# A four-layer graph kernel: last two tiles of the attention layer taken block by block, one combined flag, and filler products in two pauses

## What is computed

```python
Wh = x @ W;  f1 = Wh @ a1;  f2 = Wh @ a2
e = leaky_relu(f1 + f2.T, 0.2)
att = softmax(where(adj > 0, e, -9e15), axis=-1)
x = layernorm(x + relu(att @ Wh))          # layer 2
# layer 3: products of (adj > 0), (adj < 0) and adj with x, then with weights
```

## Time and profile before

| | |
|---|---|
| median of 3 runs | 1427.51 us (1426.62 to 1429.61) |
| the profiled execution's own time | 1426.91 us |
| its span (first to last instruction) | 1425.2 us |
| mean granted clock of TensorE | 0.977 of 2.4 GHz |
| PE busy with products | 1332.1 us, 93% |
| PE idle between layer 2 and layer 3 | 6.08 us |
| PE idle before the turns of layer 2 | 6.29 us |
| PE idle before the first tile of layer 2 | 5.73 us |

### The profile page before, as it was taken

One profiled execution on the slowest core, in us unless ns is written; L12 is line 12 of the kernel. 1 busy time (PEld: TensorE's weight loads), 2 busy tenths in 40 slices (PEclk: granted clock), 3 DMA queues, 4 the chain that ended last, 5 costly groups with the idle time before them and its releaser, 6 DMA issues.

```text
span 1425.2 us, 11729 instructions
## 1 busy us (share of the span) xinstructions
PE 1332.1 (93%) x4294; PEld 677.7 (48%) x4294; DVE 922.3 (65%) x1277; ACT 554.7 (39%) x491; POOL 193.4 (14%) x211
## 2 busy tenths in 40 slices
PE   5889997899989999999999999999999999999993
PEld 4434444344444444455445455544445444544451
DVE  6978887888864000003225453799978987898576
ACT  7543324966730000000211111456565566455343
POOL 0000002000020000000000000225430233124211
PEclk8999997999999999999999999999999999999997
DMA  9899972000026667658667158698877987688301
GB/s 396 331 389 412 391 305 99 0 0 0 0 97 187 194 195 193 193 151 268 197 219 235 35 171 308 256 371 307 313 263 256 338 314 290 240 309 319 138 1 50
DMA packets 78150, 311.10 MB, mean 218 GB/s; under 512 B 8700, under 2 KB 20603, under 8 KB 61307
## 3 DMA queue, kind: packets, MB, share of 16 engines
q1 hardware_dynamic: 78075, 310.17, 61.2%
HBM read 306.71 MB, written 3.43 MB: 218 GB/s over the span
## 4 chain that ended last, share of the span: by engine, by line
PE 83%; DMA 7%; DVE 7%; ACT 2%; issue 1%; POOL 0%; ACTq 0%; DVEq 0%; POOLq 0%; SPq 0%
PE ps L1440 30%; PE ps L1241 10%; PE ps L1175 10%; PE ps L1278 10%; PE ps L1100 6%; DMA ring<-in_adjR 6%; PE ps L1235 5%; PE ps L1350 2%; PE ps L1461 1%; DVE arena L1560 1%; PE ps L1422 1%; PE ps L1259 1%; PE ps L1462 1%; DMA ring<-in_adjB 1%; PE ps L1215 1%; PE ps L1260 1%
## 5 line engine op out<-in xcount | busy, mean ns | idle before, releaser
L1440 PE MATMUL ps<-arena,x 128*128 128x512 f32 (+1 forms) x1092 | 438.9, 562 | 2.9 <-ACT shared L978 1.6
L1440 PEld LDWEIGHTS ps<-arena,x 128*128 128x128 f32 x1092 | 206.1, 190 | 231.4 <-issue 225.2
L971 ACT ACTIVATE arena<-arena,bench 128x3328 f32<-128x3328 bf16 x78 | 239.8, 3075 | 188.8 <-PE ps L1440 176.4
L2145 DVE TENSOR_TENSOR arena<-arena,ring 128x3328 f32<-128x3328 f32 x51 | 184.7, 3621 | 26.6 <-ACT arena L971 26.1
L1241 PE MATMUL ps<-ring,x 128*128 128x512 f32 (+1 forms) x364 | 176.1, 566 | 0.0
L1278 PE MATMUL ps<-ring,x 128*128 128x512 f32 (+1 forms) x364 | 149.5, 563 | 1.3 <-DMA ring<-in_adjB 1.3
L1100 PE MATMUL ps<-ring,bench 128*128 128x512 f32 x260 | 122.7, 607 | 15.0 <-DMA ring<-in_adjR 15.0
L1845 DVE SCALAR_TENSOR_TENSOR bench<-b,cols,ps 128x128 f32<-128x128 f32 x26 | 7.3, 344 | 182.1 <-PE ps L1215 182.1
L715 POOL TENSOR_TENSOR ring<-ring,nid 128x128 f32<-128x128 f32 x51 | 95.1, 1864 | 210.8 <-DMA ring<-in_adjR 210.8
L1235 PE MATMUL ps<-arena,shared 128*128 128x512 fp8e4 (+1 forms) x364 | 103.6, 366 | 6.1 <-DVE shared L1650 6.1
L2145 DVE TENSOR_TENSOR arena<-arena 128x3328 f32<-128x3328 f32 x27 | 98.0, 3631 | 13.5 <-ACT arena L971 13.1
(11 more groups left out here) (326 smaller groups left out, 1513.4 us busy)
## 6 DMA issues: line engine op xcount, KB each, us to landing
ring<-in_adjR SPq DMA_DIRECT2D x51, 1664.0 KB, 8.7
ring<-in_adjB SPq DMA_DIRECT2D x312, 256.0 KB, 3.0
arena<-in_adjR SPq DMA_DIRECT2D x27, 1664.0 KB, 8.8
ring<-in_adjR SPq DMA_DIRECT2D x25, 1280.0 KB, 8.5
shared<-in_adj SPq DMA_DIRECT2D x7, 1664.0 KB, 10.8
es<-in_adj SPq DMA_DIRECT2D x7, 1664.0 KB, 10.6
xT<-in_adj SPq DMA_DIRECT2D x6, 1664.0 KB, 13.3
y<-in_adj SPq DMA_DIRECT2D x6, 1664.0 KB, 13.1
```

Source lines behind the costliest of these rows:

```text
L971: A_(E[n % 3], below[n % 3], ACT.Exp, bias=tt_[:, t * HEADS + k:t * HEADS + k + 1], scale=-WIN).then_inc(e_exp, 1)
L1440: last = mm(ps[:, b, 0:w], lhsT=x[:, t], rhs=E[n % 3][:, o_:o_ + w], start=(t == 0), stop=(t == TILES - 1))
L2145: v.tensor_tensor(E[n % 3], E[n % 3], row_at(n), ALU.mult).then_inc(q_ready, 1)
```

## The change

It has four parts.

1. **Last two tiles.** Tiles 0 to 23 (`BY_TILE`) are taken as before. Tiles 24 and 25 are taken together, block by block, and behind each block from the second on stand two pairs of the W1 products. ACT makes all seven copies to `UT` and does its pairs in between (`RELU_BEHIND`). The buffers change place so that `shared` and the first half of the ring are free two and three tiles before the end. SP loads the first 6 chunks (`EARLY_CHUNKS`) after tile 22. POOL puts back the borrowed column of `x` in two pieces. `PART1` goes from 12 to 8 tiles, and only every other step of DVE's loop has a `norm_pair`.
2. **One flag.** DVE also computes the smaller of both flags (`BOTH`). PE asks that one before layer 2. If it is set, layer 2 and the start of layer 3 follow each other without another question and without a jump.
3. **Filler products before the turns:** 5 products of 512 columns into bank 3, whose results nobody reads, behind layer 1's last product.
4. **Filler products before layer 2:** 4 products into bank 7, behind the flag and POOL's `aside_done`.

```diff
-        EL = [piece(ring_flat, 0, NP), piece(ring_flat, NP, NP), es_flat, shared[:]]
+        turned_tile = [piece(ring_flat, 0, NP), piece(ring_flat, NP, NP)]
+        EL = [es_flat, turned_tile[1], turned_tile[0], shared[:]]
...
-        PART1, PART2 = 12, 24
+        PART1, PART2 = 8, 24
+        BY_TILE = TILES - 2
+        RELU_BEHIND = ((), (0, 1), (2, 3), (4, 5), (6, 7), (8,), (9, 10, 11, 12))
+        EARLY_CHUNKS = NP // CW
...
-        Z1_BANKS = (7, 0, 1, 2, 3, 4, 5, 7, 1, 3, 4, 5, 6)
+        Z1_BANKS = (7, 0, 1, 7, 2, 7, 3, 1, 4, 7, 5, 3, 6)
...
@@ SP, layer2 @@
+                    sp.wait_ge(used1, TILES - 3)
+                for t in range(EARLY_CHUNKS):
+                    ring_load(R2, t, 0, t, BLOCKS[0][1])
+                if not general:
                     sp.wait_ge(sums1, NB)
...
@@ ACT, layer2 @@
+                act.wait_ge(used1, BY_TILE)
                 for b, (o_, w) in enumerate(BLOCKS):
+                    act.wait_ge(sums1, b + 1)
+                    A_(UT[:, o_:o_ + w], ps[:, b, 0:w], ACT.Identity, bias=xsb).then_inc(ut1, 1)
+                    for k in RELU_BEHIND[b]:
+                        relu_pair(k)
+                        if k == PART1 // 2 + 1:
+                            roots(1, 0, PART1)
...
@@ PE, behind layer 1's products @@
+            def keep_busy(bank, rhs, times):
+                for _ in range(times):
+                    mm(ps[:, bank, :], lhsT=ident[:], rhs=rhs, start=True, stop=True)
+
+            keep_busy(3, xT[:, 0:MAX_WIDTH], 5)
...
@@ PE, layer2 @@
+                def products1(lo, hi):
+                    for k in range(lo, hi):
+                        pe.wait_ge(ut1, max(k // 2, Z1_BANKS[k] if Z1_BANKS[k] < NB else 0) + 1)
+                        if Z1_BEFORE[k] is not None:
+                            pe.wait_ge(z_out, 2 + GROUPS + Z1_BEFORE[k] + 1)
...
                     if t == 0:
                         pe.wait_ge(aside_done, 2)
+                        keep_busy(7, x[:, 0:BT].rearrange("p t f -> p (t f)"), 4)
...
+                for b, (o_, w) in enumerate(BLOCKS):
+                    for t in range(BY_TILE, TILES):
+                        if b == 0:
+                            pe.wait_ge(q1, t)
+                        op = mm(ps[:, b, 0:w], lhsT=x[:, t], rhs=EL[t % 4][:, o_:o_ + w], start=False, stop=(t == TILES - 1))
+                    op.then_inc(sums1, 1)
+                    if b:
+                        products1(2 * b - 2, 2 * b)
+                products1(GROUPS - 1, GROUPS)
-            either(pe, after_layer2, 0)
+
+            def all_usual(otherwise):
+                if otherwise:
+                    either(pe, layer2, 1)
+                    either(pe, after_layer2, 0)
+                else:
+                    layer2(False)
+                    after_layer2(False)
+            either(pe, all_usual, BOTH, ready=2)
...
@@ DVE, span flag at t == 16 @@
-                    v.tensor_scalar(flag[0:1, 1:2], spans[0:1, 0:1], spans[0:1, 1:2], SPAN, ALU.add, ALU.is_le).then_inc(flag_ready, 1)
+                    step(v.tensor_tensor(row[0:1, 2:3], spans[0:1, 0:1], spans[0:1, 1:2], ALU.add))
+                    v.tensor_scalar(flag[0:1, 1:2], row[0:1, 2:3], SPAN, None, ALU.is_le)
+                    v.scalar_tensor_tensor(flag[0:1, BOTH:BOTH + 1], row[0:1, 2:3], SPAN, flag[0:1, 0:1], ALU.is_le,
+                                           ALU.min).then_inc(flag_ready, 1)
...
-                    if k > PART1 // 2 + 1:
-                        norm_pair(k - PART1 // 2 - 2)
+                    if k > PART1 // 2 + 1 and (k - PART1 // 2) % 2 == 0:
+                        norm_pair((k - PART1 // 2 - 2) // 2)
```

More of the change, by code:

```diff
@@ L444, in is_, with either @@
             return isinstance(g, int) and g == k
-        def either(eng, section, which):
-            eng.wait_ge(flag_ready, which + 1)
+        def either(eng, section, which, ready=None):
+            eng.wait_ge(flag_ready, ready or which + 1)
             usual = eng.value_load(flag[0:1, which:which + 1], min_val=0, max_val=1)
@@ L673, in layer2, with add_pairs @@
                 g_.memset(x[:, :, F - 1:F], 1.0).then_inc(aside_done, 1)
[L674 to L680, removed]
+                def add_pairs(lo, hi):
+                    for k in range(lo, hi):
+                        pool.wait_ge(z_out, 2 + GROUPS + k + 1)
+                        g_.tensor_tensor(y[:, 2 * k:2 * k + 2], hb4[:, 2 * (k % 2):2 * (k % 2) + 2], x[:, 2 * k:2 * k + 2],
+                                         ALU.add).then_inc(y_done, 1)
+                for n, (lo, hi) in enumerate(((0, BY_TILE), (BY_TILE, TILES))):
+                    if n == 0:
+                        pool.wait_ge(used1, BY_TILE)
+                    else:
+                        pool.wait_ge(sums1, NB)
+                    g_.tensor_copy(x[:, lo:hi, F - 1:F], aside[:, lo:hi, None]).then_inc(aside_done, 1)
+                    pool.wait_ge(aside_done, 3 + n)
+                    add_pairs(lo // 2, hi // 2)
             either(pool, layer2, 1)
@@ L1174, in layer2 @@
                             pe.wait_ge(q1_part, 1 if b == 0 else 2)
[L1175 to L1188, removed]
-                    op.then_inc(z_done, 1)
-            either(pe, layer2, 1)
+                        op = mm(ps[:, b, 0:w], lhsT=x[:, t], rhs=EL[t % 4][:, o_:o_ + w], start=(t == 0), stop=False)
+                    op.then_inc(used1, 1)
+                for b, (o_, w) in enumerate(BLOCKS):
[7 more added lines that the diff above has]
+                products1(GROUPS - 1, GROUPS)
             def heads_vectors():
@@ L1831, in layer2_and_norm @@
                 variances(2 * GROUPS, PART1, TILES)
-                for c in range(0 if general else GROUPS - PART1 // 2 - 2, PART1 // 2):
+                for c in range(0 if general else PART1 // 2, PART1 // 2):
                     norm_pair(c)
@@ L2245 @@
 FR_READY = 20
[L2246 to L2252 removed]
+GAP_READY = 23
+BACK_READY = 24
+XSB_READY = 28
+V6_READY = 37
+B2_READY = 38
+LATE_READY = 43
+GS_READY = 56
 MX_READY = 3
```

40 lines of the change are left out of this document (12 added, 28 removed).

## The result

| | before | after |
|---|---|---|
| median | 1427.01 us (6 runs, 1425.01 to 1429.61) | 1415.51 us (6 runs, 1411.25 to 1418.67) |
| ratio of the times | | 0.9919, 95% interval 0.9905 to 0.9934 |
| the profiled execution's own time | 1426.91 us | 1414.20 us |
| its span | 1425.2 us | 1412.5 us |
| mean granted clock | 0.977 | 0.988 |

The page of the kernel after answers to the earlier trace rows: busy time by engine, and the chain's shares.

What follows compares the result with a forecast made beforehand. The prediction took PE, busy for 93% of the span, to bound the kernel. Terms 6.8 + 2.2 + 1.2 + 0.7 = 10.9 us off 1426.9 left 1416.0, plus 0.6 for the median: 1416.6 us, range 1413.5 to 1421.

Steps and rivals of the forecast that it cites:

- The pause before layer 3: Border of layers 2 and 3: PE goes straight on at 417.7 instead of 424.53, worth 6.8 us.
- The walk: Block-by-block count of the engines from tile 24's start at 399.45, putting the end of PE's products at 417.7.
- Tile 25's wait: In the new tail, PE waits 0.6 us for tile 25's scores from DVE.
- The half clock behind it: Layer 3's first two tiles: without a pause they take 2.6 us at full clock, not 4.8, worth 2.2 us.
- The reading of the gap: Pause before layer 3: PE's own jump, flag load and branch, with its instruction fetch waiting behind the chunks, not x16.
- load and branch cost something more: Pause before layer 3: fetch alone would allow a start at about 421.8; load and branch explain the row of 424.53.
- Fillers before tile 0: Start of layer 2: full clock ends tile 0 at 266.3, but tile 1's scores come at 267.4; worth 1.2 us.
- Fillers before the turns: Behind layer 1's last product: a higher clock in the turns, between -0.35 and +1.4 us, taken as 0.7 us.
- The flag on DVE: One more waited step and one more operation before the gap ACT waits for, costing about 0.35 us.
- What is late next: Layer 3's pair 4 from DVE: wanted at 428, done at 426.3, a margin of 1.7 us.
- The rival of the tail's queue: PE waits at each of the last three blocks or pair 4 is late: 3.5 us lost, 1420; chance 0.12.
- The slower rival: Tail: short products and waits lose the clock, 13 us lost against 10.9 gained, 1429.6; chance 0.05.

Runs made afterwards that it cites:

- before_half_chunks: The kernel before, with SP issuing only 6 of layer 3's 13 first chunks after the last sum, 7 once all pairs are out; 1423.90 us, one run.
- jump_only: The changed kernel, but PE asks layer 2's flag alone, jumps across its general version and starts layer 3 without a second question; 1419.42 us, one run.
- near_question: The changed kernel plus one flag question with two empty versions between the last W1 pair and layer 3; 1419.86 us, one run.
- no_fillers: The changed kernel without both groups of filler products; 0.9943 of the kernel before, median 1416.38 us.
- flag_only: The kernel before with the combined flag alone, old tail order and x16, no fillers; 0.9976 of the kernel before.
- two_questions: The changed kernel with PE asking its two flags one after the other again, so the jump before layer 3 returns; 0.9981 of the kernel before.

## Why the prediction was right, step by step

- **The pause before layer 3, 6.8 us.** 6.89. The walk put the end of the products at 417.7 (it started from 399.45; the row has 399.55, which makes 417.8); with the trace's start 3.0 us sooner this is 414.7 to 414.8, and it was 414.80. Tile 25's wait shows as 0.36 us of idle time, and from start to start it costs 397.93 - 396.54 - 0.86 = 0.53 of the 0.6. ACT's last copy shows as 0.23 and costs 413.19 - 412.37 - 0.43 = 0.39 of the 0.4.
- **The half clock behind it, 2.2 us.** 2.05 by the timelines. The forecast took its 4.8 us from the chain, where the third tile stands at 429.32 and not at 429.16.
- **The reading of the gap.** The packet behind the chunks was right (before_half_chunks), and so was that removing the jump alone leaves the `x16` wait: alone it gives 3.4 us, and it costs 8.8 us to put it back. The step that failed is "load and branch cost something more": a question is 0.3 to 0.9 us. Of the 3.4 us between the packet's start (421.10) and 424.53, 1.03 are the packet itself, 1.50 stand behind a landing without any question (jump_only), and 0.9 are the question's. This did not touch the forecast, which took the whole gap as gone.
- **The Trainium skill's rule** ("Runtime: NRT & Kernel Launch", "Instruction fetch mechanics": a taken branch out of the fetched pages waits for a fetch by DMA) holds here: near_question 0.56 us, jump_only 3.68 us. By that rule I gave 421.8 as the earliest start, and before_half_chunks, with the fetch out of the chunks' way, started at 421.87, held by `x16`.
- **Fillers before tile 0, 1.2 us.** 1.25, and 1.3 against no_fillers, and what ends it is tile 1's scores, as forecast. The question ahead of them cost 0.30 us of the 0 to 2.7 that I had bounded, so they ended 1.63 us early.
- **Fillers before the turns, 0.7 us.** 0.32 against before in the profiled execution (0.5 against no_fillers, which has the flag's steps too), 1.3 against before where the clock stays. The sign that I gave for this part, a clock of 1.00 in the stretch from 242, did not come (0.62). The case I left out is that the clock may not have fallen when they start; then they end 2.5 us early and it falls afterwards. The term of 0.7 lies between the two cases, and that the sum came out with it is in part luck.
- **The flag on DVE, 0.35 us.** About 0.13.
- **What is late next.** DVE was right as the next, but its margin was mis-sized: I gave 1.7 us at pair 4, and it was 0.1. Two steps of its loop took 3.1 us and not 2.8. Single operations stretched, L1684 from 0.43 to 0.93 us at 410.88, where one of POOL's adds runs (410.81 to 411.53), and to 0.83 at 414.07 (an add from 413.73 to 414.61), but not at 417.57, beside none. That the adds are the cause was not tried. The rival of the tail's queue was closer than its chance says.
- **The slower rival** did not come: the tail ran at 1.00.

## What to carry to other kernels

A far jump in the stream of the engine that sets the pace cost 3.68 us here, 4.7 to 4.8 with a question, and 6.08 to 7.67 where its fetch stood behind bulk transfers, so ask once, early, where the engine waits anyway. This pause had several causes that end close together: the flag alone gave 3.4 us, fillers alone 1.9, and flag, early `x16`, early chunks and interleaving together the whole pause and the clock behind it. In each of these kernels what was late next, and not the length of the pause, decided what the edit gave.

## What the runs showed of the hardware that I had not expected

- Putting PE's fetch behind 13 chunks of 256 KB and not 6 delayed its packet by 2.6 us (421.10 against 418.46) at a DMA share near 1. With the queue just begun it was 1.2 to 1.6 us later than with free engines, measured from PE's last product (1.15 to 1.51 against -0.07).
- The stop of PE for 3.35 us in flag_only was followed by half clock at the restart (0.50 at 420).
- The point where layer 1 ends stands between 238.1 and 246.7 us in traces of kernels whose DVE does the same work up to there. A part of this is the transfers of the first stage: in two_questions, the latest, PE waits 3.6 us longer for them than in the kernel after (19.2 against 15.6), and the rest was not traced. The spread is larger than most terms of this study; distances between two points of one trace are the safer measure.
